# A graph-attention layer on one core: second scores two units behind their first instead of three

## The reference, cut to what matters

```
feats  = einsum('bnf,hfo->bhno', x, kernel)
scores = einsum('hbnd,hbdm->hbnm', f_self, f_other)      # f_self, f_other: projections of x
masked = a * scores
masked = where(masked >= 0, masked, 0.2 * masked) / sqrt(16)
attn   = softmax(masked + where(a == 0, -1e9, 0)) * where(a == 0, 0, 1)
out    = relu(einsum('bhnm,bhmo->bhno', attn, feats) + bias)   # heads side by side: 64 values
result = layernorm(x + out)
```

## Time and profile before

| | |
|---|---|
| time, median of 3 runs | 906.92 us (906.81 to 907.31) |
| the profiled execution | 912.7 us, span from first to last instruction 910.8 us |
| mean granted TensorE clock | 0.964 |
| PE busy | 835.0 us, 92% |
| ACT busy | 780.0 us, 86% |
| DVE busy | 774.7 us, 85% |
| POOL busy | 657.8 us, 72% |

### The profile page before, as it was taken

The page is one execution under the profiler, slowest core; times in us unless marked ns, Lnnn a source line. Parts: engine busy times, 40 slices in busy tenths (PEclk is TensorE's granted clock), DMA queues, the critical chain, the costliest instruction groups (busy, mean ns, idle before and its releaser), DMA issues.

```text
span 910.8 us, 14879 instructions
## 1 busy us (share of the span) xinstructions
PE 835.0 (92%) x4668; PEld 259.5 (28%) x4668; DVE 774.7 (85%) x1422; ACT 780.0 (86%) x1553; POOL 657.8 (72%) x643
## 2 busy tenths in 40 slices
PE   4079998999989999999999999899999999899993
PEld 3022332233323332233323332232322333222220
DVE  3176998889978899989999899799999899899993
ACT  2078997899978999999989999799999999799992
POOL 5065886758877698858888599676888589766654
PEclk9589999899999999999999999999999999999996
DMA  9794689908798098935898098962999278990301
GB/s 239 136 233 123 120 187 221 239 8 218 122 257 196 0 249 160 264 119 119 192 254 227 1 233 130 265 163 52 235 203 245 57 199 137 243 196 18 48 1 36
DMA packets 198402, 144.57 MB, mean 159 GB/s; under 512 B 177104, under 2 KB 177104, under 8 KB 198320
## 3 DMA queue, kind: packets, MB, share of 16 engines
q1 hardware_dynamic: 195152, 139.91, 66.2%
q10 hardware_dynamic: 3168, 3.67, 2.4%
HBM read 94.08 MB, written 12.51 MB: 117 GB/s over the span
## 4 chain that ended last, share of the span: by engine, by line
PE 77%; DMA 7%; DVE 5%; ACT 3%; SPq 3%; issue 2%; POOL 2%; ACTq 1%; POOLq 0%; DVEq 0%
PE z L536 45%; PE numer L567 26%; DMA maskT<-mask 3%; SPq L239 3%; DVE z L850 2%; PE misc L471 2%; ACT probs L766 2%; DMA parts_dram<-part 2%; PE misc L511 1%; PE misc L477 1%; DMA w_val<-in_L_gnn_kernel 1%; SPq L231 1%; DVE probs L850 1%; PE misc L464 1%; ACT squares L707 1%
## 5 line engine op out<-in xcount | busy, mean ns | idle before, releaser
L850 DVE SCALAR_TENSOR_TENSOR z<-z,maskT 128x512 f32<-128x512 f32 (+1 forms) x864 | 557.4, 678 | 62.4 <-PE z L536 54.9
L536 PE MATMUL z<-self_st,other_st 96*128 96x512 bf16 (+3 forms) x2016 | 521.1, 381 | 39.7 <-issue 24.1
L386 POOL TENSOR_TENSOR probs<-probs,lows 128x512 f32<-128x512 f32 (+1 forms) x288 | 360.5, 1252 | 220.3 <-ACT probs L760 211.0
L766 ACT ACTIVATE probs<-z 128x512 f32<-128x512 f32 (+1 forms) x864 | 462.6, 602 | 52.0 <-PE z L536 43.2
L536 PEld LDWEIGHTS z<-self_st,other_st 96*128 96x128 bf16 (+1 forms) x2016 | 169.8, 98 | 494.4 <-ACT probs L766 223.1
L567 PE MATMUL numer<-probs,vals 128*32 128x512 f32 (+1 forms) x2304 | 304.8, 601 | 3.0 <-POOL probs L386 2.8
L850 DVE SCALAR_TENSOR_TENSOR probs<-z,maskT 128x512 f32<-128x512 f32 (+1 forms) x288 | 191.0, 663 | 41.3 <-PE z L536 25.5
L759 ACT ACTIVATE lows<-z 128x512 f32<-128x512 f32 (+1 forms) x288 | 177.3, 616 | 43.7 <-DVE probs L850 43.0
L760 ACT ACTIVATE probs<-probs 128x512 f32<-128x512 f32 (+1 forms) x288 | 187.1, 650 | 0.0
L344 POOL TENSOR_SCALAR mask<-edges 128x1500 int16<-128x1500 f32 x96 | 138.6, 1444 | 10.4 <-DMA edges<-in_adj 2.7
L567 PEld LDWEIGHTS numer<-probs,vals 128*32 128x32 f32 x2304 | 45.6, 108 | 98.9 <-ACT probs L766 75.4
(11 more groups left out here) (70 smaller groups left out, 270.2 us busy)
## 6 DMA issues: line engine op xcount, KB each, us to landing
edges<-in_adj SPq DMA_DIRECT2D x88, 750.0 KB, 5.8
parts_dram<-part SPq DMA_DIRECT2D x21, 384.0 KB, 7.0
self_st<-parts_dram SPq DMA_DIRECT2D x42, 192.0 KB, 5.6
other_st<-parts_dram SPq DMA_DIRECT2D x42, 192.0 KB, 5.8
edges<-in_adj SPq DMA_DIRECT2D x8, 468.8 KB
x_sb<-in_x SPq DMA_DIRECT2D x8, 352.0 KB
out<-cent SPq DMA_DIRECT2D x8, 352.0 KB
maskT<-mask SPq DMA_TRANSPOSE x96, 6.0
```

The source lines that it names most:

```text
L386: pool.tensor_tensor(p, p, lows[:, g % 2, 0:WIDTH[st]], ALU.mult).then_inc(pooled, 1)
L536: return nc.tensor.matmul(z[:, v % BUFS * STEP + i, 0:WIDTH[st]], other_st[par][rows, h, c * P:(c + 1) * P], self_st[par][rows, h, st * W: ...
L766: nc.scalar.activation(slot, bank, ACT.Exp, scale=LOW).then_inc(expd, 1)
L850: return nc.vector.scalar_tensor_tensor(out, z[:, v % BUFS, 0:WIDTH[st]], FLOOR, maskT[(par + st) % 2][:, c, 0:WIDTH[st]], ALU.max, ALU.mult)
```

## The change

`LIFT_LAG` goes from 3 to 2, and `ORDER` is rewritten so that the list still fits.

```
-LIFT_LAG = 3
+LIFT_LAG = 2
-ORDER = (("s", 0), ("l", 0), ("s", 1), ("l", 1), ("s", 2), ("l", 2), ("v", 0), ("s", 3))
+ORDER = (("s", 0), ("l", 0), ("s", 1), ("s", 2), ("l", 1), ("v", 0), ("s", 3), ("l", 2))
```

## The result

The changed kernel takes 902.62 us (median of 20 runs, 899.33 to 913.70). The kernel before, on the same chip, takes 910.09 us (20 runs, 903.86 to 920.01). The ratio is 0.992, with a 95% interval of 0.990 to 0.994: 7 us faster, where 1.9 were forecast. The ratios leave out the runs that lie over 1.5% above the fastest of their kernel, here two of the 20 of each. The profiled execution took 900.9 us in place of 912.7. Medians of different measurements differ (the kernel before had 906.92 in three runs, 910 to 915 in others), so I compare by ratios to runs on the same chip.

A forecast was written before the change was run, and what follows sets the result against it. PE was taken to bound plain groups at its own pace, with s0 waiting in the first stage. Gains of 3.5 us less 1.6 lost at batch beginnings made -1.9: 906.92 to 905.0 us, range 901.5 to 910.0.

The forecast's parts named there:

- Plain groups: Groups without other work: the new order costs nothing there, hidden by DVE's margin of 0.38 us on s0.
- E: Rival: DVE's 0.38 us margin on s0 is missing where finishing steps disturb it, l3 waits; 914.6 us, chance 0.04.
- Preparation: First stage's groups 7 to 12, preparing the next batch: s0's waits go, 0.50 us a batch, 3.5 us gained.
- A batch's beginning: Behind the stop for masks PE has six matmuls up to l3 instead of five: 1.6 us lost (0.3 to 3.0).
- The masks: Masks' DMA row: a first stage 0.5 us shorter starts it 0.5 us earlier, so the gain is kept.
- F: Rival: shorter first stages bring the masks' DMAs forward, some of the 15.8 us of waits goes; about 902, chance 0.10.
- B: Rival: masks land when they did, the 3.5 us become waiting at batch starts, the loss stays; 908.5 us, chance 0.17.
- C: Rival: ACT's total bounds groups 8 to 12, an earlier l1 only moves its idle time; 908.5 us, chance 0.06.
- D: Rival: PE stands 0.22 us longer at each batch's beginning and its clock falls more often; 911.2 us, chance 0.10.

The follow-up runs named there:

- with masks in time: Mask transposes issued ahead of the edge loads in a batch's last stage: on the kernel before 892.08 us (0.976), on the changed kernel 896.16 us (0.981).
- the halves: Kernel before with only one exchange, transposes and loads in old order: s0 and l1 910.82 us (1.000), s1 and l2 912.93 us (1.004).
- s0 and l1 alone: Kernel before with only the exchange of s0 and l1, transposes and loads in their old order: 910.82 us, ratio 1.000.
- l1 put off: Changed kernel with the l1 of a batch's last group run behind the next batch's first s0: 907.83 us, ratio 0.992.
- moving the landing alone: Kernel before with one edge load, the third of a batch's last stage, moved behind the fourth mask transpose: 897.40 us, ratio 0.985.

## Why the prediction was right in sign and too small

*Plain groups: right.* 2.62 us, DVE's 0.57 and PE's 1.70 unchanged; l3 waits for nothing new, so E did not come there. It came, small, where it was said to be possible: finishing steps bring DVE off its beat, and second scores wait (0.36 us in the group of the root's seed, 0.31 in the second stage's eighth).

*Preparation: the mechanism right, the size wrong.* All three waits of s0 in groups 10 to 12 and the one of group 7 ahead of the round are gone, and ACT's gap with them. But of the forecast 0.50 us a batch the stage kept 0.14 (33.86 to 33.72), 1.0 us in seven in place of 3.5. I let DVE's row end the gain, and took DVE's short steps at the lengths they had. In the group of the root's seed L916 went to 1.01 us (3.39 in place of 2.88 us for that group), and L902 at 699.96 to 0.88 (the eighth group 3.65 for 3.48). The second stage, which I had counted as unchanged, lost 0.21 in the same way.

*A batch's beginning: wrong in mechanism, and under-priced.* I priced one more matmul behind the stop, 1.6 us in all, and counted three beginnings at low clock where the trace of before has four (586.4 us is at 0.50 too); the lower bound of 0.3 holds four beginnings at 0.07, and all seven make 0.5. What the order costs there is the register load and branch, which l1 no longer leaves room for: 8.88 in place of 8.26 us with masks in time, 0.6 a batch or 4.3 in seven. I had not followed PE's own non-matmul instructions past the place where l1 now waits.

*The masks: the step that failed.* I wrote that a shorter first stage starts the DMA row earlier and that I counted nothing else there. The stage was shorter by 0.14 only, and the row from POOL's first mask for the third stage to the landing took the same within its scatter (57.4, then 57.1 and 57.3). But the need moved 1.6 us back, so the masks' lateness fell from 2.5 to 0.6 us, and the low stretches behind late beginnings went from four to one. With the ratios, on a kernel of 910 us: before with masks in time 0.976, so the masks cost 22 us (910 x 0.024); after 0.992 against 0.981, 11 us. The order lost 4.4 us (0.981 less 0.976) and the masks and the clock gave back 11.5. That is F's time, to which I gave 0.10, and not by F's way. The sign was luck: with the masks in time the order that I called faster is slower. So is it that 902.62 lies in the range: the range reached 5.4 us below the 906.92 that I started from (901.5), and against the 910.09 measured beside it the change is 7 us. The prediction's B and C did not come; of D the opposite happened: fewer stops, fewer low stretches. (The rule put beside D, from the Trainium skill, page "TensorE: Matmul & The Clock Gate", section "HAM oscillation — how this bites in real kernels", is told there of waits for DMAs that are longer than D's 1.7 us; that every stop is a risk was my reading of it.) Over all runs the mean granted clock agrees: 0.968 in 28 runs of the kernel before and 0.971 in 12 of the changed one on one chip (0.968 and 0.963 for the halves), and within those 28 the time falls as the clock rises (correlation -0.76).

*Left open.* Why the masks land 1.1 to 1.3 us later with s0 and l1 alone than with both exchanges, at nearly the same need, I did not settle, nor why l1 put off gains 0.8% at before's need and mean lateness. Landings scatter by 2 to 5 us from batch to batch within each of these traces, so seven landings of one trace hardly tell 57.2 from 58.4; but twelve runs each gave the ratios of 1.000 and 0.992, so these times are not one trace's luck. The changed kernel's gain is therefore shown to lie in the masks' lateness and the clock: with the masks in time it is gone, and moving the landing alone brings it and more. The way in which the order brings it about is not shown. The later need is real, but the run with s0 and l1 alone has it without the gain, and the run with l1 put off has the gain without it. That both exchanges together narrow the spread of the landings fits the rows of these traces and was not tested.

## What to carry to other kernels

Where a transfer lands within a few microseconds of its need, measure "landing less need" at each place first, and not only its mean: a reordering of an engine that has nothing to do with it can win or lose there, and moving one load behind what is waited for may give more than the reordering. Judge an order with that wait taken away, or its own sign stays hidden: this one gains 0.8% and is slower in itself by 0.5%. Before a semaphore-waiting instruction is moved to the end of a loop body, look for the loads and branches that ran in its shadow.

## What the runs showed of the hardware that was not expected

DVE's steps on 4 or 12 elements a partition (L902, L914, L916, L919) take 0.16 us alone and 0.70 to 1.16 where they start inside POOL's L386 of 1.28, up to its end, while DVE's 512-wide masks, which read PSUM, are not lengthened (0.68 to 0.70 either way).

A stop of PE at a batch's beginning was followed by a lower clock or was not, at nearly the same length. PE's idle time was 1.62, 1.70, 1.73, 2.14 and 2.36 us with a stretch at 0.50 behind it, and 1.59, 1.61 and 2.51 us without one. The six stops of 2.8 to 4.1 us in the traces of before, of l1 put off, and of s0 and l1 alone were all followed by one. Runs of one kernel differ, too: those of the kernel before lie 16 us apart, and that this comes from such stops is suggested by the correlation above and not shown.
